# A two-layer gated cross-attention kernel: SyncE's loads of the context and stores of x in the second attention stage, interleaved in another way

## The chip, the core and the metric

The kernel runs on one core of a Trainium2 chip. Its time is the device time of one execution in microseconds, and the number that counts is the median of several. A core has five engines with instruction queues of their own: TensorE (PE; its weight loads are shown apart, as PEld), VectorE (DVE), ScalarE (ACT), GpSimd (POOL) and SyncE (SP). Each works off its queue in order; semaphores tie the queues together. SyncE computes nothing here. It waits for semaphores and issues DMAs, and a wait in its queue holds back everything behind it.

## What is computed

The input is x, 16 batches of 100 rows by 256, and a context of 16 x 361 x 256. Four sublayers follow each other, each with a layernorm in front and a gated residual behind:

```python
x = x + tanh(g_xattn[0]) * L0_xattn(layernorm(x), ctx, ctx, ...)
x = x + tanh(g_ffn[0])   * L0_ffn(layernorm(x), ...)      # 8 experts, top 2
x = x + tanh(g_xattn[1]) * L1_xattn(layernorm(x), ctx, ...)
x = x + tanh(g_ffn[1])   * L1_ffn(layernorm(x), ...)      # 15 experts, top 3, one shared
```

The change is in the third. There queries, keys and values of 16 heads of 16 are made of x; the same queries also meet keys and values made of the context:

```python
qkv = x @ Wqkv + bqkv
qkv_a = xa @ Wqkv_aux + bqkv_aux          # xa: the 361 rows of context
dots, dots_aux = q @ k.T * scale, q @ ka.T * scale
h_main, h_aux = softmax(dots) @ v, softmax(dots_aux) @ va
out = h_main * (1 - gate) + h_aux * gate  # gate = sigmoid(g), one per head
return out @ Wo + bo
```

## The kernel before

Each sublayer is a stage: a function with its own buffers, a block of five instruction streams, and a barrier at its end. The second attention stage is `attend1`. It goes over the 16 batches in **turns** t = -2 ... 17 and works on several batches in each turn. In a full turn TensorE does, in this order:

- `turn_max(t)`, a single matmul (L926), with which a turn starts; then `by_query(t + 1, 0)` (L960), scores with one query in a row, of which VectorE takes the maxima
- `project_key(t + 2, 0)` (L934): the keys of the context of batch t + 2. It waits on `ctx_loaded` for the load of that context, and for the bank that `take_value_own(t - 1)` of VectorE (L731) has freed
- `by_key(t, 0)` (L970 and L976), scores with one key in a row, for the exponents on ScalarE. It uses banks again that the first half of `maxima(t + 1, 0)` (L703 and L704 on VectorE) must have read
- `project_key(t + 2, 1)` (L934), `by_query(t + 1, 1)` (L960), and then the rest: sums over the probabilities of batch t - 1, turns of the sums of t - 2, projections of x of t + 2 (L949), the values of the context of batch t (`values01` and `values2`, L1006), `turn_mix(t - 2)` (L1030), `project_out(t - 2)` and `values_own(t)` (L1006)

`values2(t)` is the last reader of the context of batch t; it signals `ready["value2"]`. VectorE's `residual(t - 2)` (L753) follows `project_out(t - 2)` in the same turn and signals `x_ready`. At the end of turns 2 and 6 (and of turn -2) VectorE also does `moments` for four batches of a later group (L668, L672, L676). TensorE is then already at the first matmuls of the next turn, so in the rows these steps stand at the start of turns 3 and 7.

A context is 361 KB and goes into one of NC = 4 buffers. SyncE issues the first four ahead of its loop. The loop has one step for each batch b: `load_context(b + 4)`, which waits until `values2(b)` is done (`need(sp, ready["value2"], b - NC + 1)`, called with the batch that is loaded), then a wait for `x_ready` of batch b, then the store of x of batch b (L634). Nothing in this stage reads what is stored; the stage ends when all 16 stores have landed.

Of the kernel before, what the change touches and what calls it, by code (L numbers as in the profile page):

```python
# [29 lines left out]
B, T, D = 16, 100, 256  # L30
# [12 lines left out]
def on(b):  # L43

    return not isinstance(b, int) or 0 <= b < B


def need(eng, sem, value):

    if not isinstance(value, int) or value > 0:  # L50
        eng.wait_ge(sem, value)
# [483 lines left out]
def attend1(nc, consts, x_in, x_out, ctxT, Wqkv, bqkv, Wqkv_a, bqkv_a, Wo, bo, g):  # L535

    ident, mhalf, tanhg = consts
    with ExitStack() as ctx:
# [5 lines left out]
        NC, NK, NX = 4, 3, 3  # L544
# [12 lines left out]
        xs = m.sb("x", [T, B, D])  # L557
# [23 lines left out]
        xhat_ready, x_biased, x_ready, x_stored = (m.sem(n) for n in ("xhat_ready", "x_biased", "x_ready", "x_stored"))  # L581
# [19 lines left out]
        with nc.Block() as block:  # L601
            @block.sync
            def _(sp):
                def load_context(b):
                    need(sp, ready["value2"], b - NC + 1)
                    sp.dma_start(ctxt[b % NC][:, :, :], ctxT[b].rearrange("(c p) s -> p c s", p=P)).then_inc(ctx_loaded[b % NC], 16)

                def load_x(g):
                    sp.dma_start(xs[:, g * GB:(g + 1) * GB, :], x_in[g * GB:(g + 1) * GB].rearrange("b t d -> t b d")).then_inc(x_loaded[g], 16)

                load_x(0)
                load_context(0)
                w_rows, wa_rows = (a.rearrange("(c p) n -> p c n", p=P) for a in (Wqkv, Wqkv_a))
                sp.dma_start(wa[:, :, 0:D], wa_rows[:, :, D:2 * D]).then_inc(wa_loaded, 16)
                sp.dma_start(w[:, :, 0:2 * D], w_rows[:, :, 0:2 * D]).then_inc(w_loaded, 16)
                with nc.allow_non_contiguous_dma("one bias a partition"):
                    sp.dma_start(bqk[:, :], bqkv[0:2 * D].rearrange("(c p) -> p c", p=P)).then_inc(w_loaded, 16)
                    sp.dma_start(bka[:, :], bqkv_a[D:2 * D].rearrange("(c p) -> p c", p=P)).then_inc(wa_loaded, 16)
                load_context(1)
                for tile, src in ((gexp, g), (bvb, bqkv[2 * D:3 * D]), (bvab, bqkv_a[2 * D:3 * D]), (bob, bo)):  # L620
                    sp.dma_start(tile[:, :], src.partition_broadcast(P)).then_inc(rest_loaded, 16)
                sp.dma_start(w[:, :, 2 * D:3 * D], w_rows[:, :, 2 * D:3 * D]).then_inc(rest_loaded, 16)
                sp.dma_start(wa[:, :, D:2 * D], wa_rows[:, :, 2 * D:3 * D]).then_inc(rest_loaded, 16)
                load_context(2)
                load_x(1)
                sp.dma_start(wo[:, :, :], Wo.rearrange("(c p) n -> p c n", p=P)).then_inc(rest_loaded, 16)
                load_context(3)
                for g_ in range(2, NG):
                    load_x(g_)
                for b in range(B):  # L630
                    if b + NC < B:
                        load_context(b + NC)
                    sp.wait_ge(x_ready, b + 1)
                    sp.dma_start(x_out[b], xs[:, b, :]).then_inc(x_stored, 16)  # L634
                sp.wait_ge(x_stored, 16 * B)

            @block.gpsimd
# [1166 lines left out]
```

## Time and profile before

| | us |
|---|---|
| median of 3 runs | 1506.66 (1506.36 to 1506.88) |
| the profiled execution | 1503.48 |
| its span, from the first to the last instruction | 1501.7 |
| PE busy in the span | 1221.7 (81%) |
| DVE, ACT, POOL busy | 628.2, 488.0, 390.9 |
| second attention stage (first load of x to the next stage's first load) | 641.24 to 1100.90 |
| its turns 3 to 13, the ones with a context loaded in the loop | 744.29 to 1047.61 |

Times in rows are microseconds from the start of the span. The span is 1.8 us shorter than the profiled execution's own time, and that is 3.2 us below the median of the runs; a difference of two spans is what carries over to the median. A row of the timeline is one engine's instructions of one line that follow each other, merged: start, length, engine, line, operation, names, how many, and in brackets for how long the engine was idle ahead of them and what ended that. In names the buffer numbers and the stage's number are left out: `at_ctx` is a context, `at_ring` one of two PSUM banks used in turn, `at_scores` the banks of the scores.

### The profile page before, as it was taken

The numbers are of one execution on the slowest core, as the hardware profiler recorded it, in microseconds if no ns is written. First come the engines' busy times: TensorE is split into PE (matmuls) and PEld (weight loads), VectorE is DVE, ScalarE is ACT, GpSimd is POOL, SyncE is SP. The second block draws the span as 40 slices with busy tenths as digits, with TensorE's granted clock in tenths as the row PEclk, the third lists the DMA queues.
The fourth block names the chain that finished last, engine by engine and source line by source line (L and its number), as shares of the span: only waits on it lengthen the run. The fifth ranks groups of instructions, "written<-read, shape, count | busy, mean of one in ns | idle before, by whom it ended". The sixth has DMA issues, their size and how long they took to land. (4 is left out here: it accounts for less than half of the span.)

```text
span 1501.7 us, 31104 instructions
## 1 busy us (share of the span) xinstructions
PE 1221.7 (81%) x11472; PEld 938.7 (63%) x11472; DVE 628.2 (42%) x1495; ACT 488.0 (32%) x1117; POOL 390.9 (26%) x419
## 2 busy tenths in 40 slices
PE   4888888743999999249888898888849998999970
PEld 3666666533999999225555555555636677888860
DVE  4666665546111111455645445455453702222215
ACT  2444444310333333123444334343415212222221
POOL 2445544420222222210000000000016213444442
PEclk9999999965999999679999899999958999999995
DMA  4011000034799987440000000000050208999965
GB/s 125 14 35 31 27 27 27 7 100 166 266 329 325 332 327 282 137 141 11 14 15 13 27 15 17 24 14 17 8 152 2 71 24 294 327 307 319 322 214 171
DMA packets 74575, 190.60 MB, mean 127 GB/s; under 512 B 10536, under 2 KB 46824, under 8 KB 66024
## 3 DMA queue, kind: packets, MB, share of 16 engines
q1 hardware_dynamic: 66264, 165.16, 33.4%
q0 software_dynamic: 8064, 22.03, 4.0%
q10 hardware_dynamic: 144, 1.97, 0.3%
q8 instruction: 73, 1.20, 0.3%
q14 instruction: 30, 0.25, 0.1%
HBM read 168.29 MB, written 20.84 MB: 126 GB/s over the span
## 5 line engine op out<-in xcount | busy, mean ns | idle before, releaser
L1585 ACT ACTIVATE ex_hT<-ex_h,ex_w 128x128 f32<-128x128 f32 x464 | 132.2, 368 | 338.7 <-PE ex_h L1654 338.7
L1654 PE MATMUL ex_h<-ex_xT,ex_w 128*128 128x128 f32 x1856 | 225.7, 278 | 0.0
L1654 PEld LDWEIGHTS ex_h<-ex_xT,ex_w 128*128 128x128 f32 x1856 | 217.9, 195 | 0.5
L1663 PE MATMUL ex_y<-ex_w,ex_hT 128*128 128x256 f32 x928 | 213.9, 379 | 0.0
L1663 PEld LDWEIGHTS ex_y<-ex_w,ex_hT 128*128 128x128 f32 x928 | 170.1, 190 | 19.7
L1332 POOL DMA_INDIRECT ex_results<-ex_yt,ex_to x84 | 82.9, 987 | 277.1 <-DVE ex_to L1527 139.1
L272 DVE TENSOR_REDUCE at_negmax<-at_scores 120x8 bf16<-120x800 f32 (+1 forms) x96 | 90.6, 985 | 85.8 <-PE at_scores L459 85.8
L864 ACT ACTIVATE at_probs<-at_scores 120x800 f32<-120x800 f32 (+2 forms) x128 | 100.5, 842 | 75.5 <-PE at_scores L976 75.5
L704 DVE TENSOR_REDUCE at_negmax<-at_scores 100x2 f32<-100x722 f32 x128 | 115.2, 900 | 0.0
L212 POOL TENSOR_TENSOR at_sum<-at_probs 120x800 f32<-120x800 f32 (+1 forms) x48 | 78.4, 1634 | 140.0 <-ACT at_probs L383 140.0
L934 PE MATMUL at_ring<-at_ctx,at_wkv_aux 128*128 128x361 f32 x128 | 60.6, 609 | 66.4 <-DMA at_bka<-in_L_xattn_bqkv_aux 38.6
L383 ACT ACTIVATE at_probs<-at_scores 120x800 f32<-120x800 f32 (+1 forms) x96 | 80.0, 835 | 102.4 <-PE at_scores L468 102.2
L703 DVE TENSOR_REDUCE at_negmax<-at_scores 100x2 f32<-100x200 f32 x128 | 46.3, 362 | 138.6 <-PE at_scores L960 138.5
L1327 POOL DMA_INDIRECT ex_xt<-ex_normed,ex_from x84 | 81.6, 972 | 73.8 <-DVE ex_from L1522 38.8
L1540 DVE TENSOR_TENSOR ex_yt<-ex_y,ex_b 128x256 f32<-128x256 f32 x32 | 13.6, 424 | 190.1 <-PE ex_y L1663 190.1
L934 PEld LDWEIGHTS at_ring<-at_ctx,at_wkv_aux 128*128 128x128 f32 x128 | 27.2, 234 | 94.6 <-issue 49.3
L960 PE MATMUL at_scores<-at_kT,at_qz 32*100 32x461 f32 x512 | 67.5, 597 | 7.2 <-DVE at_negmax L704 3.3
L970 PE MATMUL at_scores<-at_qz,at_kT 32*120 32x200 f32 (+2 forms) x1024 | 66.3, 376 | 7.4 <-DVE at_negmax L704 7.4
L459 PE MATMUL at_scores<-at_qz,at_kT 32*120 32x200 f32 (+1 forms) x768 | 45.8, 352 | 30.6 <-ACT at_probs L383 29.7
L970 PEld LDWEIGHTS at_scores<-at_qz,at_kT 32*120 32x120 f32 (+2 forms) x1024 | 45.4, 190 | 33.1 <-issue 31.9
L647 POOL TENSOR_TENSOR at_x<-at_x,at_bo 100x256 f32<-100x256 f32 x16 | 11.5, 724 | 200.1 <-DVE at_xhat L693 192.2
L459 PEld LDWEIGHTS at_scores<-at_qz,at_kT 32*120 32x120 f32 (+1 forms) x768 | 30.6, 177 | 48.8 <-ACT at_probs L383 48.5
(240 smaller groups left out, 1851.5 us busy)
## 6 DMA issues: line engine op xcount, KB each, us to landing
ex_w<-in_pack_in SPq DMA_DIRECT2D x32, 1028.0 KB, 5.7
ex_w<-in_pack_out SPq DMA_DIRECT2D x32, 1024.0 KB
ex_w<-in_pack_in SPq DMA_DIRECT2D x52, 514.0 KB, 5.0
ex_w<-in_pack_out SPq DMA_DIRECT2D x52, 512.0 KB
at_ctx<-in_ctxT SPq DMA_DIRECT2D x32, 361.0 KB, 3.5
x<-at_x SPq DMA_DIRECT2D x32, 100.0 KB
ex_x<-x SPq DMA_DIRECT2D x8, 400.0 KB
ex_normed<-ex_xhat SPq DMA_DIRECT2D x8, 400.0 KB
```

The source lines that it names most:

```text
L212: pool.tensor_tensor(sum2[0:r, :, :], p[:, :, 0:T2], p[:, :, T2:T], ALU.add).then_inc(sum2_done, 1)
L272: dve.tensor_reduce(negmax[0:r, half, :].rearrange("p (s h) -> p s h", h=HS), by_head, AX, ALU.max, negate=True).then_inc(max_done, 1)
L383: act.activation(probs[t % 2][0:r, j, half * HH:(half + 1) * HH, :].rearrange("p (s h) t -> p s (h t)", s=2), ps_s[0:r, 2 * half:2 * half ...
L704: dve.tensor_reduce(by_strip[:, :, HS + u], pair[0:T, :, T:KEYS], AX, ALU.max, negate=True).then_inc(max_done, 1)
L864: act.activation(probs[b % 2][0:r, u, half * HH:(half + 1) * HH, :].rearrange("p (s h) t -> p s (h t)", s=2), score_pair("k", b, u, half)[ ...
L934: last = pe.matmul(bank[:, 0:S], wa[:, c, i * P:(i + 1) * P], ctxt[b % NC][:, c, :], start=(c == 0), stop=(c == KC - 1))
L970: pe.matmul(score_pair("k", b, u, strip // 2)[0:r, strip % 2, i * 2 * T:(i + 1) * 2 * T], kT[b % NK][rows, i, k0:k0 + r], qz[b % NK][rows, ...
L1327: pool.indirect_dma_start(xt[s][:, :], None, xhd, bass.IndirectOffsetOnAxis(gi[s][:, :], 0)).then_inc(gathered[s], 16)
L1332: pool.indirect_dma_start(ways, bass.IndirectOffsetOnAxis(si[s][:, :], 0), yt[s][:, :], None).then_inc(scattered[s], 16)
L1585: last = act.activation(hT[s][:, c, :], ps_h[:, bank, i * P:(i + 1) * P], ACT.Gelu, bias=w1[s][:, B1 + c:B1 + c + 1])
L1654: last = pe.matmul(ps_h[:, bank, i * P:(i + 1) * P], w1[s][:, c * ff + f:c * ff + f + P], xT[s][:, c, :], start=(c == 0), stop=(c == KC - 1))
L1663: last = pe.matmul(ps_y[:, s, 0:D], hT[s][:, c, :], w2[s][:, c * D:(c + 1) * D], start=(c == 0), stop=(c == FC - 1))
```

## The change

The loop on SyncE no longer goes over batches but over t = 0 ... 17. In step t it issues the load of the context of batch t + 4 and then, where there is a batch t - 2, waits for its x and stores it. The first two steps have a load and no store, the last six a store and no load (before: the last four). Waits, transfers and their sizes are the same ones; no other engine's instructions change.

```diff
-                for b in range(B):
-                    if b + NC < B:
-                        load_context(b + NC)
-                    sp.wait_ge(x_ready, b + 1)
-                    sp.dma_start(x_out[b], xs[:, b, :]).then_inc(x_stored, 16)
+                for t in range(B + 2):
+                    if t + NC < B:
+                        load_context(t + NC)
+                    if on(t - 2):
+                        sp.wait_ge(x_ready, t - 1)
+                        sp.dma_start(x_out[t - 2], xs[:, t - 2, :]).then_inc(x_stored, 16)
                 sp.wait_ge(x_stored, 16 * B)
```

SyncE's instructions at the start of this loop, as a difference of the two programs (`x3` is the stage's output, `at1_ctx1` the buffer of the contexts of batches 1, 5, 9 and 13; the stores only move, and change their line by one):

```order
 L606 DMA at1_ctx0<-in_ctxT 128x2x361
-L634 DMA x3<-at1_x 100x256
 L606 DMA at1_ctx1<-in_ctxT 128x2x361
-L634 DMA x3<-at1_x 100x256
 L606 DMA at1_ctx2<-in_ctxT 128x2x361
-L634 DMA x3<-at1_x 100x256
+L635 DMA x3<-at1_x 100x256
 L606 DMA at1_ctx3<-in_ctxT 128x2x361
```

The loads of batches 4, 5 and 6 now stand in a row, and the store of batch 0 stands behind the load of batch 6 and no longer ahead of that of batch 5: each later load has moved past two stores.

At the end of the loop:

```order
 L606 DMA at1_ctx3<-in_ctxT 128x2x361
-L634 DMA x3<-at1_x 100x256 x5
+L635 DMA x3<-at1_x 100x256 x7
```

Behind the load of batch 15 there were five stores (batches 11 to 15) and are now seven (9 to 15).

## Rows read from the trace of the kernel before

**Rows 1.** Who waited for whom, turns 3 to 13: total us, times, longest.

```profile
PE at_ring L934 <- DMA at_ctx<-in_ctxT: 27.8, 11, 3.1
```

**Rows 2.** Busy time and granted clock of turns 2, 3, 7, 9, and of 3 to 13.

```profile
core 0: us, PE busy (x) PEld busy (x) DVE busy (x) ACT busy (x) POOL busy (x), PEclk, DMA share, GB/s
...
720.80:744.29 23.49, 22.64 (x299) 14.56 (x297) 13.48 (x28) 11.35 (x22) 0.00 (x0) 1.00 0.01 1
744.29:770.41 26.12, 22.62 (x298) 14.61 (x298) 15.25 (x37) 10.61 (x20) 3.12 (x4) 1.00 0.08 20
...
853.00:882.40 29.40, 25.46 (x299) 15.97 (x298) 15.26 (x37) 10.73 (x20) 3.12 (x4) 0.88 0.07 17
...
909.86:937.26 27.40, 24.20 (x298) 15.35 (x298) 13.48 (x28) 10.72 (x20) 0.72 (x1) 0.94 0.07 18
...
744.29:1047.61 303.32, 266.15 (x3268) 168.97 (x3268) 152.69 (x332) 117.08 (x220) 9.87 (x13) 0.94 0.07 19
```

**Rows 3.** Timeline of SyncE's queue: loads (L606) and a store (L634).

```profile
697.10 0.40 SPq L606 DMA_DIRECT2D at_ctx<-in_ctxT  x1
744.14 0.29 SPq L634 DMA_DIRECT2D x<-at_x  x1
744.48 0.39 SPq L606 DMA_DIRECT2D at_ctx<-in_ctxT  x1
```

**Rows 4.** Timeline of PE, turn 2 and the start of turn 3.

```profile
720.80 0.25 PE L926 MATMUL at_ring<-const_ident,at_negmax 100*128 100x100 f32 x1
...
721.95 1.48 PE L934 MATMUL at_ring<-at_ctx,at_wkv_aux 128*128 128x361 f32 x4
723.41 0.94 PE L970 MATMUL at_scores<-at_qz,at_kT 32*100 32x200 f32 x16
...
725.86 1.03 PE L960 MATMUL at_scores<-at_kT,at_qz 32*100 32x461 f32 x8
...
733.08 2.03 PE L949 MATMUL at_ring<-at_xT,at_wqkv 128*128 128x100 f32 x16
...
740.19 1.05 PE L1006 MATMUL at_ring<-at_wkv_aux,at_ctx 128*120 128x256 f32 x4
...
748.16 1.45 PE L934 MATMUL at_ring<-at_ctx,at_wkv_aux 128*128 128x361 f32 x4 [2.65 <-DMA at_ctx<-in_ctxT]
```

**Rows 5.** Timeline of PE, start of turn 9.

```profile
913.42 1.75 PE L934 MATMUL at_ring<-at_ctx,at_wkv_aux 128*128 128x361 f32 x4 [2.35 <-DMA at_ctx<-in_ctxT]
915.10 1.67 PE L970 MATMUL at_scores<-at_qz,at_kT 32*100 32x200 f32 x16
...
918.84 1.03 PE L960 MATMUL at_scores<-at_kT,at_qz 32*100 32x461 f32 x8
```

**Rows 6.** Timeline of DVE at the start of turns 2, 3 and 7.

```profile
722.37 0.90 DVE L704 TENSOR_REDUCE at_negmax<-at_scores 100x2 f32<-100x722 f32 x1
...
744.83 1.39 DVE L668 BATCH_NORM_STATS2 at_stats<-at_x 100x6 f32<-100x256 f32 x4
...
747.52 0.90 DVE L704 TENSOR_REDUCE at_negmax<-at_scores 100x2 f32<-100x722 f32 x1
...
856.22 0.90 DVE L704 TENSOR_REDUCE at_negmax<-at_scores 100x2 f32<-100x722 f32 x1
```

**Rows 7.** Timeline of PE in turn 0, and beside the load issued at 697.10.

```profile
683.91 0.95 PE L970 MATMUL at_scores<-at_qz,at_kT 32*121 32x200 f32 x16 [1.40 <-DVE at_negmax L704]
...
686.05 1.87 PE L960 MATMUL at_scores<-at_kT,at_qz 32*100 32x461 f32 x8 [0.70 <-ACT at_probs L864]
687.86 3.74 PE L949 MATMUL at_ring<-at_xT,at_wqkv 128*128 128x100 f32 x16
...
697.41 0.95 PE L970 MATMUL at_scores<-at_qz,at_kT 32*120 32x200 f32 x16 [0.34 <-DVE at_negmax L704]
```

**Rows 8.** Busy time and granted clock in the first expert stage.

```profile
410.00:560.00 150.00, 150.00 (x1038) 140.48 (x1038) 20.32 (x84) 46.39 (x164) 40.15 (x41) 1.00 0.90 326
```

## The prediction

> **What bounds the kernel now.** The stages follow each other behind barriers, so what the change is worth is read inside the second attention stage. I read three views there. First, who waited for whom: TensorE's keys of the context (L934) stood 11 times for the load of that context, 27.8 us in all, at most 3.1 at once [rows 1]. Then the busy times cut at the first matmul of each turn (L926): a turn is TensorE's, 22.64 us busy of 23.49 in turn 2, with VectorE at 13.48 and ScalarE at 11.35 [rows 2]. Last, the timelines, for why the load is late. In SyncE's queue the load of batch 5 stands behind the store of batch 0, which is issued at 744.14, at the end of turn 2; the load goes out at 744.48 [rows 3], and the matmuls that need it start at 748.16, in turn 3, 3.68 us after the issue, having idled 2.65 [rows 4]. The buffer it goes into was free a whole turn earlier: values2 of batch 1 is in turn 1. So the load is held back by the store ahead of it and by nothing else.
>
> Turn 2 shows the same turn without this wait. It does every step of a full turn, but its context (batch 4) was issued at 697.10 [rows 3], since the first load in the loop has no store ahead. There L934 starts at 721.95 with no idle time [rows 4]. This turn is the yardstick for turns 3 to 13.
>
> **The change part by part.**
>
> *The load leaves earlier.* The load of batch t + 4 now waits for values2 of batch t alone, and for the store of batch t - 3, one turn back. In turn 2 values2 is over at 740.19 + 1.05 = 741.24 [rows 4], which is 741.24 - 720.80 = 20.44 us into the turn. The context is asked for 1.15 us into turn t + 2 (721.95 - 720.80). From issue to need there are then 23.49 - 20.44 + 23.49 + 1.15 = 27.7 us, against the 3.68 that the load took. That the wait goes is near certain. It covers batches 5 to 15, so all 11 waits; batch 4 is loaded as before.
>
> *What a turn gains.* By the yardstick turns 3 to 13 would take 11 x 23.49 = 258.39 us and took 303.32 [rows 2]: 44.93 more. Of this 27.8 is the wait. The other 17.1 is TensorE's clock: in turn 9 the granted clock is 0.94 of full [rows 2], a mean of a stretch at 1.2 GHz and the rest at 2.4. The stretch stands right behind the idle time: L934 takes 1.75 us where it takes 1.48 in turn 2, L970 1.67 where it takes 0.94 [rows 4, 5]. Turn 9 is 27.40 - 23.49 = 3.91 longer than turn 2, 2.35 the wait and 1.56 the clock. Behind that nothing differs: from the second L960 to the end it has 937.26 - 918.84 = 18.42 us, turn 2 has 744.29 - 725.86 = 18.43 [rows 2, 4, 5]. Turn 3 had the wait and no fall of the clock (26.12 = 23.49 + 2.65 - 0.02, clock 1.00), turn 7 the dearest (29.40 - 23.49 - 3.09 = 2.82 for the clock; its wait is the longest of rows 1) [rows 1, 2]. With the wait gone its cause is gone, so I take the clock's 17.1 as gained too.
>
> *What is late next: turns 3 and 7.* TensorE can't start L970 of by_key(t, 0) until VectorE has taken the first half of the maxima of the scores ahead of it. In turn 2 that half ends at 722.37 + 0.90 = 723.27 and L970 starts 0.14 later, at 723.41, just when L934 ends (721.95 + 1.48 = 723.43) [rows 4, 6]. So the two are level in a plain turn, and there VectorE costs nothing. In turns 3 and 7 VectorE has the moments ahead of the maxima (1.39 us for the first step alone), and the half ends at 747.52 + 0.90 = 748.42 and 856.22 + 0.90 = 857.12 [rows 6]. None of this waited for the context. With 0.14 on top that is 4.27 and 4.26 us after the turns' starts, 744.29 and 853.00, against 2.61 in turn 2: 1.66 and 1.65 us of wait that the wait for the DMA had hidden. Together 3.3 us come back.
>
> *The stores.* A store of batch t - 2 stands behind the load of batch t + 4. That load waits for values2(t), over 20.44 us into turn t; the x it stores is ready later in the same turn (store issued at 744.14, 23.34 us into turn 2) [rows 3, 4]. The load needs 0.39 us to issue [rows 3], so the store keeps its time. The last stores have no load among them, before or after. Nothing for them: 0 us.
>
> *The load beside other work.* Before, it ran while TensorE stood; now it runs beside L970, L1006 and the next turn's start. The one load that already did so is that of 697.10: the L970 behind it, started at 697.41, took 0.95 us, as one in turn 0 at 683.91 with no load beside it took 0.95 [rows 3, 7]. And 150 us at 326 GB/s beside a TensorE without a gap kept the clock at 1.00 [rows 8]. So nothing here either; from above I bound it by the difference that such rows could hide, 0.01 us in some 5 groups of 11 turns, 0.6 us.
>
> *The clock, weighed against a rule.* Turn 2 has TensorE idle for 23.49 - 22.64 = 0.85 us in all, and its clock stays at 1.00 [rows 2]. The Trainium skill has a rule that speaks against counting the clock's share as gained: in "TensorE: Matmul & The Clock Gate", section "A second HAM failure mode: psum-queue depth-cycling", a kernel that cycles through PSUM banks lets TensorE go idle for moments between groups of matmuls, often enough that its clock keeps going up and down, with no wait for a DMA. This stage does cycle through two banks. By that rule the sum would be 24.5 us of gain instead of 41.6. The trace disagrees for turn 2, whose clock is 1.00.
>
> **The sum.** Gain 44.93 - 3.31 = 41.6 us. The profiled execution would go from 1503.48 to 1461.9, the median from 1506.66 to 1465.1. The profiled one was 3.2 us under the median of the runs; I let this stand for how much of the rest can shift without a cause in this stage, and apply the difference to the median.
>
> **The rivals.**
>
> *The clock falls in turns 3 and 7.* The new wait of 1.66 us for VectorE could do what the old one did. Against it: turn 3 had 2.65 us of idle time at clock 1.00 [rows 2, 4]. For it: in turn 0 idle times of 1.40 and 0.70 us were followed by matmuls at the low clock: L960 took 1.87 us (1.03 in turn 2), L949 3.74 (2.03), together 2.55 lost [rows 4, 7]. The price is 1.56 (turn 9) to 2.82 (turn 7) for each fall, so one or two of them give 1465.1 + 1.6 to + 5.6, 1466.7 to 1470.7.
>
> *The moments cost nothing.* If VectorE does them where it now idles, the 3.3 us don't come back: 1461.7. Against it, VectorE's order is fixed and they stand ahead of the maxima.
>
> *The clock keeps falling in every turn.* The mechanism: short idle times between matmul groups are enough for it once in a turn, and turn 2 was lucky. Then only the wait is gained, 27.8 - 3.3 = 24.5 us: 1482.2. The skill's rule above gives this result. Turn 2's clock of 1.00 speaks against it [rows 2].
>
> *The change doesn't do what it says.* If the load were late for another reason than its issue (the transfer itself, or the buffer), the wait would stay: 1506.7. Against it, 3.68 us from issue to use, 27.7 us of room.
>
> *Slower.* The idle time in each turn may be what lets the core hold the high clock for the rest. Place: TensorE in turns 3 to 13, then 96% busy (22.64 of 23.49) for some 260 us. Turn 7 prices it: 0.12 of 29.40 us below full share in the granted clock is twice that, 7.1 us, at 1.2 GHz, and costs 2.82, so 0.40 us for each us at the low level. From 41.6 / 0.40 = 104 us at the low level on, the kernel is slower; if all 262 us went there, 105 us would be lost, and the time would be 1465 + 105 = 1570. Against it: TensorE had no idle time at all in 150 us of the expert stage, with the clock at 1.00 [rows 8].
>
> **How the numbers follow.** Forecast 62%, 1465.1, itself good to about 1.5 us either way (the sum's roundings and the shifts of the stages behind). Clock falls in turn 3 or 7 or both: 25%. Moments free: 4%. Clock falls in every turn: 4%. No effect: 3%. Slower: 2%. The range of 8 in 10 takes the forecast, the moments' case and the falls in turns 3 and 7 to their ends: 1461.7 to 1471. A measurement of this kernel tells 0.2%, some 3 us, from no change; all but the last two cases gain more than that: faster 95%, same 3%, slower 2%.
>
> **What would show it.** In the profile after, the timeline of SyncE should have the load of batch 5 in turn 1, before 720.8, and from then on a load some 2.9 us ahead of each store. The wait of L934 for at_ctx should be gone from the waits. Turns 4, 5, 6 and 8 to 13 should take 23.5 us at clock 1.00, turns 3 and 7 25.1, with L970 idle some 1.7 us for DVE L704. The stage's turns 3 to 13 should take 261.7 us. The prediction is wrong if plain turns stay above 24 us: with the clock at 0.94 it is the case of the clock, at 1.00 a wait that turn 2 doesn't have.

## The result and the profile after

| | before | with the change |
|---|---|---|
| median | 1506.77 us (1506.36 to 1509.62, 4 runs) | 1460.94 us (1459.17 to 1463.12, 4 runs) |
| profiled execution, its span | 1503.48, 1501.7 | 1459.17, 1457.4 |
| turns 3 to 13 | 303.32 | 261.76 |

The ratio of the times is 0.9693, with an interval of 0.9675 to 0.971: the kernel is 3.1% faster. The forecast was 1465.1 with a range from 1461.7 to 1471.0. The time lies 4.2 us under the forecast and 0.8 under the range's low end.

The turns came out as forecast. These are the busy times of the changed kernel cut at the turns, columns as in [rows 2]: turns 2, 3, 4, 7 and 9, and turns 3 to 13 together.

```profile
719.14:742.63 23.49, 22.63 (x298) 14.56 (x297) 13.49 (x28) 11.35 (x22) 0.00 (x0) 1.00 0.07 20
742.63:767.79 25.16, 22.66 (x298) 14.64 (x298) 15.25 (x37) 10.63 (x20) 3.12 (x4) 1.00 0.07 20
767.79:791.29 23.50, 22.64 (x299) 14.64 (x298) 14.13 (x32) 10.63 (x20) 0.72 (x1) 1.00 0.08 23
...
838.27:863.43 25.16, 22.65 (x298) 14.63 (x298) 15.25 (x37) 10.63 (x20) 3.12 (x4) 1.00 0.07 20
...
886.92:910.41 23.49, 22.64 (x298) 14.63 (x298) 13.49 (x28) 10.63 (x20) 0.73 (x1) 1.00 0.08 21
...
742.63:1004.39 261.76, 249.06 (x3269) 161.01 (x3268) 152.66 (x332) 116.90 (x220) 9.85 (x13) 1.00 0.07 19
```

Turn 2 has not moved (23.49 as in [rows 2]). The plain turns now have its length, where turn 9 had 27.40, and the clock column says 1.00 for the whole stretch, which said 0.94. Turns 3 and 7 are the two longer ones, 25.16.

What TensorE waited for in turns 3 to 13, who waited for whom, answers to [rows 1]; this is the whole list, and the context is no longer in it.

```profile
PE at_scores L971 <- DVE at_negmax L705: 5.4, 13, 1.7
PE at_ring L1007 <- ACT at_kT L856: 5.4, 11, 0.5
PE at_ring L993 <- DVE at_mixed L742: 1.9, 11, 0.2
```

SyncE's queue after, against [rows 3]: the loads of batches 4, 5 and 6 in one merged row, then a store, then a load and a store in each turn, the load 2.87 us ahead (764.77 and 767.64). The line ahead of them is from the view of L606 alone, cut to 697.5 to 720: the load of batch 5 is issued at 716.8, in turn 1.

```profile
L606 SPq DMA_DIRECT2D at_ctx<-in_ctxT x1: 394/394/394, 716.8 to 716.8; - x1
...
695.44 44.54 SPq L606 DMA_DIRECT2D at_ctx<-in_ctxT  x3
742.48 0.32 SPq L635 DMA_DIRECT2D x<-at_x  x1
764.77 0.37 SPq L606 DMA_DIRECT2D at_ctx<-in_ctxT  x1
767.64 0.31 SPq L635 DMA_DIRECT2D x<-at_x  x1
```

And the start of turn 3 on TensorE, against [rows 4]. The keys of the context (L935; L934 in the kernel before) start 1.15 us into the turn with no idle time; L971 behind them waits 1.65 us for VectorE.

```profile
742.63 0.25 PE L927 MATMUL at_ring<-const_ident,at_negmax 100*128 100x100 f32 x1
...
743.78 1.48 PE L935 MATMUL at_ring<-at_ctx,at_wkv_aux 128*128 128x361 f32 x4
746.91 0.94 PE L971 MATMUL at_scores<-at_qz,at_kT 32*100 32x200 f32 x16 [1.65 <-DVE at_negmax L705]
```

So the profiled execution became 44.3 us shorter (1503.48 to 1459.17), of which 303.32 - 261.76 = 41.56 in these turns and 2.8 elsewhere. What the 2.8 are was the open question.

### The profile page after: what moved, and what is told of

Read it like the earlier page. It is cut to its first block and busy times, and to the rows that moved or that the text cites. A ratio compares the mean times of both kernels' runs of the same rounds, so it can differ in the third digit from the quotient of the medians.

```text
span 1457.4 us, 31104 instructions
## 1 busy us (share of the span) xinstructions
PE 1204.5 (83%) x11472; PEld 928.7 (64%) x11472; DVE 629.4 (43%) x1495; ACT 488.4 (34%) x1117; POOL 390.6 (27%) x419
## 3 DMA queue, kind: packets, MB, share of 16 engines
q10 hardware_dynamic: 144, 1.97, 0.4%
## 5 line engine op out<-in xcount | busy, mean ns | idle before, releaser
L935 PE MATMUL at_ring<-at_ctx,at_wkv_aux 128*128 128x361 f32 x128 | 51.6, 533 | 39.3 <-DMA at_bka<-in_L_xattn_bqkv_aux 39.3
L961 PE MATMUL at_scores<-at_kT,at_qz 32*100 32x461 f32 x512 | 66.9, 592 | 5.5 <-ACT at_kT L856 2.2
L971 PE MATMUL at_scores<-at_qz,at_kT 32*120 32x200 f32 (+2 forms) x1024 | 60.7, 350 | 10.7 <-DVE at_negmax L705 10.7
L935 PEld LDWEIGHTS at_ring<-at_ctx,at_wkv_aux 128*128 128x128 f32 x128 | 24.3, 209 | 64.8 <-DMA at_bka<-in_L_xattn_bqkv_aux 39.7
L971 PEld LDWEIGHTS at_scores<-at_qz,at_kT 32*120 32x120 f32 (+2 forms) x1024 | 41.6, 173 | 31.7 <-issue 31.4
```

Of the source, the lines that this page charges most:

```text
L971: pe.matmul(score_pair("k", b, u, strip // 2)[0:r, strip % 2, i * 2 * T:(i + 1) * 2 * T], kT[b % NK][rows, i, k0:k0 + r], qz[b % NK][rows, ...
```

## The experiments

**The pair once more.** Both kernels unchanged.

> The changed kernel once more, for its median and for a second profile cut into stretches: start to the second attention stage, its first turns, turns 3 to 13, the rest of the stage, the last expert stage. Turns 3 to 13 took 261.76 us in the first profile. Theory (what the time gained beyond the forecast comes from work that the change doesn't touch, and varies from run to run): turns 3 to 13 again at 261.8, each of the other stretches off its first value by up to 2 us, the median between 1459 and 1466. Rival (the change gains 3 to 4 us outside these turns as well, always): the same stretches again below those of the kernel before by the same amounts, in sum by 2.7 us, and a median of 1461 or less.

> The kernel before once more, as the other half of that comparison. Both theories: turns 3 to 13 at 303 to 304 us (11 waits for the context, 28 us, and the clock at 0.94). Theory of shifting stretches: the time outside these turns, 1200.2 us of profiled execution in the first profile against 1197.4 in the changed kernel's, moves by up to 3 us either way. Rival: it stays 2.7 us above that of the changed kernel.

Measured: 1460.24 us (1456.91 to 1462.53, 5 runs) for the changed kernel and 1503.87 (1498.29 to 1508.9, 12 runs) for the one before; the reference runs of the kernel before on the same chip gave 1507.13 (1499.73 to 1512.38, 17 runs). Turns 3 to 13 took 261.78 and 303.12 us. The part of the span outside them was 1194.7 and 1196.9, a difference of 2.2 us, and the median of 1460.24 lies in the range of either theory, so this pair didn't decide between them. One thing stands out: executions of the kernel before lie up to 14 us apart. The three runs shown ahead of the prediction lay within 0.5.

**Half of the move.**

```diff
-                for t in range(B + 2):
+                for t in range(B + 1):
                     if t + NC < B:
                         load_context(t + NC)
-                    if on(t - 2):
-                        sp.wait_ge(x_ready, t - 1)
-                        sp.dma_start(x_out[t - 2], xs[:, t - 2, :]).then_inc(x_stored, 16)
+                    if on(t - 1):
+                        sp.wait_ge(x_ready, t)
+                        sp.dma_start(x_out[t - 1], xs[:, t - 1, :]).then_inc(x_stored, 16)
```

> The changed kernel with only half of the move: SyncE issues the load of batch t + 4 ahead of the store of batch t - 1, so that each load stands behind the store of the batch two turns back and is issued at the end of one turn for the start of the next but one. My theory (the load needs 3.7 us of lead, and one turn of 23.5 is plenty): turns 3 to 13 at 261.8 us as in the changed kernel, time within 0.2% of it, some 1461 us. Rival (the second store ahead of the load mattered too, by delaying loads or by colliding with the store): waits of L935 for at_ctx of 1 us or more in each turn, 1472 us or more.

Measured: 1461.99 us (1459.66 to 1466.0, 4 runs), ratio to the kernel before 0.9706 (0.9682 to 0.973); turns 3 to 13 at 261.80. SyncE's queue has the load right behind the store again, as before the change, but the load is now for a batch that is needed a turn later:

```profile
772.55 0.31 SPq L635 DMA_DIRECT2D x<-at_x  x1
772.91 0.37 SPq L606 DMA_DIRECT2D at_ctx<-in_ctxT  x1
```

It makes no difference. Moving each load past one store instead of two gives the whole gain; the rival falls.

**The moments, moved to where VectorE idles.**

```diff
                         normalize(t - 2, 1)
                         mix_up(t - 2)
+                    if t % GB == GB - 2 and (t + 2) // GB + 1 < NG:
+                        moments((t + 2) // GB + 1)
                     if on(t):
                         take_values01(t)
...
                     if on(t):
                         take_value_own(t)
-                    if t % GB == GB - 2 and (t + 2) // GB + 1 < NG:
-                        moments((t + 2) // GB + 1)
```

> The changed kernel with VectorE's moments for a group of four batches moved from the end of turns 2 and 6 to the middle of them, right behind mix_up, where VectorE idles 2.1 us for the values of the context; they take 2.0 us there. My theory (the moments are what turns 3 and 7 wait for, 1.65 us each): turns 3 and 7 at 23.5 us as the others, turns 3 to 13 at 258.4, 3.3 us less than the changed kernel, some 1457.6 us. Rival (the wait for VectorE in these turns has another cause, or returns in turns 2 and 6): no change, 1461.

Measured: 1457.35 us (1452.18 to 1458.76, 5 runs), ratio to the kernel before 0.9681 (0.9659 to 0.9702). Turns 2 and 3, and turns 3 to 13, from the same view:

```profile
718.61:742.10 23.49, 22.64 (x298) 14.56 (x297) 15.36 (x37) 11.34 (x22) 2.40 (x3) 1.00 0.07 20
742.10:765.59 23.49, 22.64 (x298) 14.63 (x298) 13.49 (x28) 10.62 (x20) 0.72 (x1) 1.00 0.08 22
...
742.10:1000.55 258.45, 249.06 (x3269) 161.00 (x3268) 151.12 (x323) 116.75 (x220) 7.46 (x10) 1.00 0.07 19
```

The moments have gone from turn 3 (VectorE busy 13.49 us, 15.25 in the changed kernel) to turn 2 (15.36, 13.49 there), which is no longer for it; turn 3 is a plain turn. In VectorE's timeline they fill the wait for the values of the context, which was 2.15 us in the changed kernel and is 0.20 now:

```profile
734.69 1.40 DVE L669 BATCH_NORM_STATS2 at_stats<-at_x 100x6 f32<-100x256 f32 x4
736.13 0.38 DVE L673 BATCH_NORM_AGGREGATE at_mv<-at_stats 100x2 f32<-100x6 f32 x4
736.54 0.17 DVE L677 TENSOR_SCALAR at_var<-at_mv 100x4 f32<-100x4 f32 x1
736.92 0.76 DVE L720 TENSOR_TENSOR at_va<-at_ring,at_bv_aux 121x256 f32<-121x256 f32 x2 [0.20 <-PE at_ring L1007]
```

261.8 - 258.45 = 3.3 us, the forecast's term for turns 3 and 7. This is the fastest version here, though its whole times overlap those of the changed kernel; the 3.3 us are read from the turns.

**The wait without the DMA.** Two kernels, both the changed one with a wait for VectorE ahead of the keys of the context in turns 3 to 13 (+ 2 for the long one, + 1 for the short one):

```diff
                     if i == 0:
                         pe.wait_ge(ctx_loaded[b % NC], 16 * (b // NC + 1))
+                        if b >= 5:
+                            pe.wait_ge(max_done, (b - 1) * UNITS * HALVES + 2)
```

> The changed kernel with a wait put back that has nothing to do with a DMA: in turns 3 to 13 TensorE's project_key(t + 2, 0) waits until VectorE has taken both halves of the maxima of by_query(t + 1, 0). That is 3.55 us into a plain turn, so TensorE idles about 2.5 us there, as long as it did for the context, and 4.2 us in turns 3 and 7, while the context has long landed. My theory (the low clock came from the idle time): clock 0.94 in these turns again, 1.6 us lost to it in each, 27.6 us for a plain turn, turns 3 to 13 at some 306 us, 1505 us in all. Rival (the low clock came from the load or its lateness, not from TensorE's idle time): clock 1.00, plain turns at 26.0, turns 3 to 13 at 290, 1489 us.

> The same with a shorter wait: project_key(t + 2, 0) waits for the first half of these maxima alone, 2.47 us into a plain turn, so TensorE idles about 1.5 us there and 3.1 us in turns 3 and 7. If idle times of 1.5 us leave the clock as it is (as in turns 3 and 7 of the changed kernel): plain turns at 24.95, turns 3 to 13 at 278, some 1477 us. If they bring it down in every turn: plain turns at 26.5, turns 3 to 13 at 297, some 1497 us.

The long one gave 1510.02 us (1504.85 to 1515.02, 10 runs), 0.39% above the kernel before on its chip (0.17 to 0.61). Its turns 3, 4, 12 and 13 and turns 3 to 13, and the start of turn 4 (the two new lines put L935 at L937 and L971 at L973):

```profile
746.93:776.85 29.92, 24.92 (x299) 15.74 (x298) 15.25 (x37) 10.66 (x20) 3.12 (x4) 0.89 0.06 18
776.85:804.44 27.59, 24.25 (x298) 15.33 (x298) 14.13 (x32) 10.62 (x20) 0.72 (x1) 0.94 0.07 19
...
999.63:1028.65 29.02, 25.68 (x299) 16.12 (x298) 13.25 (x27) 10.72 (x20) 0.00 (x0) 0.88 0.02 5
1028.65:1056.19 27.54, 24.21 (x299) 15.47 (x298) 13.25 (x27) 10.72 (x20) 0.00 (x0) 0.94 0.02 6
...
746.93:1056.19 309.26, 269.22 (x3269) 170.39 (x3268) 152.69 (x332) 117.06 (x220) 9.85 (x13) 0.92 0.06 16
```

```profile
780.54 2.29 PE L937 MATMUL at_ring<-at_ctx,at_wkv_aux 128*128 128x361 f32 x4 [2.49 <-DVE at_negmax L705]
782.77 1.67 PE L973 MATMUL at_scores<-at_qz,at_kT 32*100 32x200 f32 x16
```

The plain turn is 27.59 with 2.49 of wait: 27.59 - 23.49 - 2.49 = 1.61 for the clock, as in turn 9 before (1.56). The loads are early here and nothing waits for one; in turns 12 and 13 no load of a context is issued at all (the last one goes out at 996.61, in turn 11; 5 and 6 GB/s), and the clock falls in them too. The low clock came from TensorE's idle time, whoever caused it; the rival (26.0 at clock 1.00) falls. The eleven turns are 3 us longer than the 306 expected: turns 3 and 7 lost 29.92 - 23.49 - 4.15 = 2.28 us each to the clock and turn 12 lost 29.02 - 23.49 - 2.49 = 3.04, where 1.6 had been put down for each. The profiled execution, 1515.02, was the longest of the ten.

The short one gave 1480.49 us (1474.17 to 1487.31, 4 runs), ratio 0.9867 (0.9823 to 0.9911). Turns 3 and 4 and all eleven, and the start of turn 4:

```profile
742.48:770.60 28.12, 24.20 (x298) 15.47 (x298) 15.25 (x37) 10.72 (x20) 3.12 (x4) 0.94 0.07 18
770.60:795.48 24.88, 22.63 (x298) 14.61 (x298) 14.12 (x32) 10.62 (x20) 0.73 (x1) 1.00 0.08 21
...
742.48:1022.61 280.13, 252.04 (x3268) 162.25 (x3268) 152.71 (x332) 116.99 (x220) 9.86 (x13) 0.99 0.06 18
```

```profile
773.21 1.45 PE L937 MATMUL at_ring<-at_ctx,at_wkv_aux 128*128 128x361 f32 x4 [1.40 <-DVE at_negmax L705]
774.60 0.94 PE L973 MATMUL at_scores<-at_qz,at_kT 32*100 32x200 f32 x16
```

With 1.40 us of wait the clock stays at 1.00 and L973 takes 0.94, though the added instruction is the same as in the long one; in turns 3 and 7, where the wait is 3.1, it falls and costs 28.12 - 23.49 - 3.06 = 1.57. The profile has the 278 us of the first case plus these two falls. The median is 3.5 us above that case's 1477, and the four executions lie 13 us apart; only the fastest was profiled, so what the slower ones lose is not shown.

**Four more profiles of the kernel before.** Unchanged kernel.

> First of four more profiles of the kernel before, to see how far its own turns 3 to 13 vary. All runs so far together put the change at 44.6 us (medians 1504.86 of 46 and 1460.31 of 9), the turns in the first pair of profiles at 41.6. Theory (the two profiled executions of the kernel before had its turns at their cheapest: in others some turns lose 2.8 us to the clock, as turn 7, and not 1.6): turns 3 to 13 between 303 and 309 us over the four, 305 or more in the mean, and the rest of the span about the same for both kernels. Rival (the turns always take 303.2 us, and the 3 us lie outside them): all four at 303.0 to 303.5, and the rest of the span 3 us longer than the changed kernel's 1195.

> Second of four profiles of the kernel before. Theory: turns 3 to 13 between 303 and 309 us, with one to three turns of 28.7 us or more beside turn 7. Rival: 303.0 to 303.5, as in the two profiles so far.

> Third of four profiles of the kernel before. Theory: turns 3 to 13 between 303 and 309 us, with one to three turns of 28.7 us or more beside turn 7. Rival: 303.0 to 303.5, as in the two profiles so far.

> Fourth of four profiles of the kernel before. Theory: turns 3 to 13 between 303 and 309 us, with one to three turns of 28.7 us or more beside turn 7. Rival: 303.0 to 303.5, as in the two profiles so far.

**Four more profiles of the changed kernel.** Unchanged kernel.

> First of four more profiles of the changed kernel. Turns 3 to 13 at 261.8 us in each. For the stretch from the stage's first load to turn 1: theory (where the clock falls in it is a matter of the moment, which differs between executions of either program): values between 54.8 and 58 in these four, some of them at 57 or more, mean 56 to 58. Rival (the difference comes with the program, from how its instructions lie): 54.8 to 55.0 in at least three of four, mean below 55.5.

> Second of four profiles of the changed kernel. Turns 3 to 13 at 261.8 us. From the stage's first load to turn 1: theory of the moment: anywhere from 54.8 to 58. Rival (comes with the program): 54.8 to 55.0.

> Third of four profiles of the changed kernel. Turns 3 to 13 at 261.8 us. From the stage's first load to turn 1: theory of the moment: anywhere from 54.8 to 58. Rival (comes with the program): 54.8 to 55.0.

> Fourth of four profiles of the changed kernel. Turns 3 to 13 at 261.8 us. From the stage's first load to turn 1: theory of the moment: anywhere from 54.8 to 58. Rival (comes with the program): 54.8 to 55.0.

All profiles of the two kernels, cut into stretches from the timelines, in us. "First" is from the stage's first load of x to turn 1, "last" from the next stage's first load to the end, "rest" all of the span but turns 3 to 13.

| | first | turns 1, 2 | turns 3 to 13 | last | rest |
|---|---|---|---|---|---|
| before, first profile | 58.2 | 44.88 | 303.32 | 400.8 | 1198.4 |
| r_before | 58.1 | 44.89 | 303.12 | 398.4 | 1196.9 |
| b_prof1 | 56.1 | 44.89 | 302.65 | 402.7 | 1201.9 |
| b_prof2 | 61.2 | 44.89 | 302.83 | 397.6 | 1198.3 |
| b_prof3 | 58.4 | 44.90 | 302.16 | 399.1 | 1199.7 |
| b_prof4 | 56.4 | 44.90 | 306.60 | 395.8 | 1192.6 |
| after, first profile | 54.8 | 44.88 | 261.76 | 399.1 | 1195.6 |
| r_after | 54.8 | 44.89 | 261.78 | 399.0 | 1194.7 |
| a_prof1 | 55.2 | 44.89 | 261.81 | 404.9 | 1201.2 |
| a_prof2 | 58.3 | 44.88 | 261.78 | 400.2 | 1201.4 |
| a_prof3 | 59.4 | 44.89 | 261.80 | 398.1 | 1202.7 |
| a_prof4 | 56.3 | 44.89 | 261.76 | 396.6 | 1196.1 |

What follows:

- In the kernel before, turns 3 to 13 took 302.2 to 306.6, 303.4 in the mean; the four new profiles have 303.6, not the 305 or more that I expected of them. The rival's 303.0 to 303.5 holds for none of the four.
- The fall that costs more, with the clock at 0.88, does not belong to turn 7. Four profiles have it there (29.3 to 29.5 us). In b_prof1 it is turn 4, and turn 7, with as long a wait (2.92), has 0.94. In b_prof4 it is turns 3 and 9, and turn 7 has 28.20 us at 0.94; as turn 3 loses nothing in the other five, this is the one profile with a longer sum. What decides where it falls is not shown. Turns 4 and 7 of b_prof1, then turns 3 and 9 of b_prof4:

```profile
771.38:800.58 29.20, 25.64 (x298) 16.14 (x298) 14.14 (x32) 10.72 (x20) 0.72 (x1) 0.88 0.07 18
855.43:883.45 28.02, 24.25 (x298) 15.30 (x298) 15.27 (x37) 10.61 (x20) 3.12 (x4) 0.94 0.07 18
...
744.11:773.30 29.19, 25.66 (x299) 16.11 (x298) 15.27 (x37) 10.73 (x20) 3.13 (x4) 0.88 0.06 18
...
911.47:940.52 29.05, 25.69 (x299) 16.11 (x298) 13.50 (x28) 10.74 (x20) 0.72 (x1) 0.88 0.06 17
```

- The mean gain in these turns is 303.45 - 261.78 = 41.7 us, forecast 41.6.
- The rest of the span is 1198.0 in the mean before and 1198.6 after, each moving over 8 to 9 us. The six profiles of either kernel thus show no gain outside these turns, but with such a spread the difference of the two means is itself uncertain by some 4 us: the 3 us of the rival are made unlikely, and 1 or 2 us that come with the change are not excluded. The four last profiles of each kernel were also taken on different chips, and what the chip adds is not separated.
- The first stretch looked like such a difference as long as it had been seen twice or three times (54.8 against 58). It isn't one. The four new profiles of the changed kernel have 55.2 to 59.4, 57.3 in the mean, as the theory of the moment has it (59.4 is above its 58), and the rival's 54.8 to 55.0 in none. In a_prof2 L961 and L950 run at the low clock behind an idle time of 1.08 us and take 1.87 and 3.74 us; behind one of 1.07 us the same two ran at the full clock in the first profile of the changed kernel, 1.03 and 2.03. That is 2.55 of the 3.5 us between the two stretches. First the changed kernel's first profile, then a_prof2, timeline of PE:

```profile
669.73 1.03 PE L961 MATMUL at_scores<-at_kT,at_qz 32*100 32x461 f32 x8 [1.07 <-DVE at_negmax L705]
670.70 2.03 PE L950 MATMUL at_ring<-at_xT,at_wqkv 128*128 128x100 f32 x16
```

```profile
671.35 1.87 PE L961 MATMUL at_scores<-at_kT,at_qz 32*100 32x461 f32 x8 [1.08 <-DVE at_negmax L705]
673.15 3.74 PE L950 MATMUL at_ring<-at_xT,at_wqkv 128*128 128x100 f32 x16
```

- Over all executions of the two kernels, the mean is 1504.7 before (52 of them, 1498.3 to 1512.5) and 1461.4 after (13, 1456.9 to 1466.2): a gain of 43.3 us, uncertain by 1.8. The 41.7 of the turns lie within that.
- Of the stretches outside turns 3 to 13 the last stage moves most, 395.8 to 404.9 us. It isn't part of the change. TensorE was busy for 327.53 us of it at clock 0.89 in a_prof1, the longest, and for 321.53 at 0.91 in b_prof4, the shortest; what else moves it is not shown.

## Why the prediction was right or wrong

**The load leaves earlier: right.** All 11 waits are gone. Half the move does the same, so the 27.7 us of room were far more than needed.

**The turn's gain by the yardstick of turn 2: right.** Plain turns take 23.49 to 23.51 in all six profiles, clock 1.00. That the clock's share comes back with the wait was an inference from order in time; the long idle wait showed it, by bringing the low clock back with no load involved. That turn 7 is the dearest was a reading of one profile: two of the six have it elsewhere.

**Turns 3 and 7: right.** 1.65 us of wait each for the first half of the maxima, 25.16 long (forecast 25.1). Moving the moments took this away (261.8 to 258.45).

**The stores, the load beside other work: right.** The store of batch 0 is issued 742.48 - 719.14 = 23.34 us into turn 2, as before; TensorE's busy time in plain turns is 22.64 with the load beside it.

**The clock and the rule weighed against it.** The rival that turn 2 was lucky did not come true in any turn of six profiles. The Trainium skill's rule ("TensorE: Matmul & The Clock Gate", section "A second HAM failure mode: psum-queue depth-cycling"), by which frequent short idle moments between groups of matmuls keep the clock going up and down, does not hold for the turns of this kernel. 0.85 us of idle time a turn in small pieces, and even one piece of 1.40 us more, left the clock up; one of 2.49 us brought it down. That turns 3 and 7 of the changed kernel, with 1.65 us, might lose the clock was given 25%; they kept it in all six profiles.

**The sum for the whole kernel: its size right, its uncertainty and its base wrong.** The step that failed is in the part on how the numbers follow: "itself good to about 1.5 us either way", and with it the low end of 1461.7, which was the case of free moments with no allowance for anything else. I had three runs within 0.5 us and a profiled execution 3.2 us below them, saw the latter as a sign that the rest shifts, and did not widen the range by it. The runs showed a spread of 3.5 us (one standard deviation) for the kernel before and 2.8 for the one after. The base was off as well: 1506.66 was a median of three, and 52 executions have their mean at 1504.7. From there the same sum gives 1504.7 - 41.6 = 1463.1, against a mean of 1461.4 for 13. Of the 4.2 us that the prediction missed, 1504.7 against 1506.66 is 2.0; the rest is within what a median of four executions can be off, and no run traces it to a cause. The pair of the result, 1506.77 and 1460.94, shows a gain of 45.8 us, where all executions together show 43.3. No term for turns 3 to 13 was mis-sized by more than 0.1 us.

## What to carry to other kernels

In a queue that both prefetches and stores, look at what each load stands behind: here a load whose buffer had long been free waited for the store ahead of it, and issuing it one store earlier was enough. If the trace has a turn in which the wait doesn't occur (here turn 2, whose load had no store ahead), its length is the yardstick for the others; here it forecast them to a tenth of a microsecond, once what else that wait had covered was added back. Price the gap in TensorE by what the clock does behind it, too: here mostly 1.6 us behind a wait of about 2.5 us, and 2.8 to 3.1 us in seven of 66 turns. And take the range from how far whole executions lie apart, not from three that happen to agree.

## What the runs showed of the hardware

An idle time of 1.40 us between groups of matmuls in an otherwise full turn left the granted clock at 1.00 in all nine plain turns of the short idle wait, and one of 1.65 us did in turns 3 and 7 of all six profiles of the changed kernel. In the long idle wait, 2.49 us brought it to 1.2 GHz for a stretch of each of the nine plain turns. In the kernel before, 61 of 66 waits for the context, 1.97 to 3.12 us long, were followed by such a stretch (the shortest in turn 6 of b_prof3: 27.09 us at clock 0.94). The five that were not, 2.52 to 2.65 us, are all in turn 3 (26.0 to 26.1 us); in the sixth profile turn 3, with 2.67, lost it as well (29.19). So the length of the idle time alone does not decide.

In the first turns of the stage, where idle times are many, the place where the clock falls moved between executions of the same program. The stretch up to turn 1 took 54.8 to 59.4 us in six profiles of the changed kernel and 56.1 to 61.2 in six of the kernel before, which is part of what sets executions of one program 9 to 14 us apart.
